# Another order for the tasks of a head pair, on five in-order engines

## The reference

```python
def attention(x, Wq, Wk, Wv, Wp, bp, rel_table):          # 16 heads of 64
    bias = rel_table[clip(rel + 16, 0, 32)]                # rel = key position - query position
    q, k, v = (einsum('btc,hcd->bhtd', x, W) for W in (Wq, Wk, Wv))
    scores = q @ k.T / sqrt(64) + bias                     # causal mask
    return (softmax(scores) @ v).reshape(B, T, 1024) @ Wp + bp

def ffn(x, W_r, W_k, W_v, mu_r, mu_k):
    x_prev = x shifted by one token
    xr, xk = mu_r * x + (1 - mu_r) * x_prev, mu_k * x + (1 - mu_k) * x_prev
    return sigmoid(xr @ W_r.T) * (square(relu(xk @ W_k.T)) @ W_v.T)

x = x + layernorm(attention(layernorm(x), ...))
x = x + layernorm(ffn(layernorm(x), ...))
```

## Time and profile before

| | before |
|---|---|
| median of 3 runs | 2538.27 us (2537.19 to 2540.73) |
| the profiled execution | 2540.03 us |
| its span, first to last instruction | 2538.2 us |
| TensorE products busy | 2326.0 us, 92% |
| VectorE busy | 1971.8 us, 78% |
| ScalarE busy | 1652.5 us, 65% |
| GpSimd busy | 1494.0 us, 59% |
| mean granted TensorE clock | 0.979 |
| chain that ended last | PE 63%, DVE 16%, ACT 13%, issue 7% |

### The profile page before, as it was taken

How to read it: one execution, slowest core, us unless ns; L and a number is a source line. 1 busy time by engine, 2 the same in 40 slices (tenths; PEclk the granted TensorE clock), 3 DMA queues, 4 the chain that set the end, 5 groups by cost and what they waited for, 6 DMA issues and landing times.

```text
span 2538.2 us, 81004 instructions
## 1 busy us (share of the span) xinstructions
PE 2326.0 (92%) x29568; PEld 1533.4 (60%) x29568; DVE 1971.8 (78%) x3848; ACT 1652.5 (65%) x2524; POOL 1494.0 (59%) x2593
## 2 busy tenths in 40 slices
PE   3888989999999999999999999999999999999886
PEld 1454556666656666666666666666666666666575
DVE  6777777888878888788887878778888887777746
ACT  2576666666766766666666676676676666666653
POOL 2233335666666676676666666666667665555652
PEclk8899989999999999999999999999999999999998
DMA  6011111111111111111111111111111111111130
GB/s 156 26 39 39 37 45 49 53 52 59 58 55 56 48 52 58 59 54 58 52 53 50 60 54 61 55 47 52 61 58 54 58 51 48 50 54 53 55 111 20
DMA packets 182457, 140.35 MB, mean 55 GB/s; under 512 B 10400, under 2 KB 173088, under 8 KB 182048
## 3 DMA queue, kind: packets, MB, share of 16 engines
q1 hardware_dynamic: 182048, 134.98, 17.4%
HBM read 57.81 MB, written 43.06 MB: 40 GB/s over the span
## 4 chain that ended last, share of the span: by engine, by line
PE 63%; DVE 16%; ACT 13%; issue 7%; DMA 0%; DVEq 0%; ACTq 0%; POOL 0%; POOLq 0%
PE score_ps L606 12%; PE misc L689 8%; PE misc L562 7%; ACT probs_f L953 6%; DVE row_max L1212 5%; PE misc L670 5%; PE max_ps L628 5%; PE misc L672 4%; PE misc L671 4%; PE misc L577 4%; PE score_ps L610 4%; DVE probs L1196 3%; ACT probs L971 2%; DVE score_ps L1228 2%; PE misc L714 2%
## 5 line engine op out<-in xcount | busy, mean ns | idle before, releaser
L1583 POOL TENSOR_TENSOR probs<-probs_f,probs 128x1024 f16<-128x1024 f32 (+1 forms) x320 | 616.5, 1934 | 517.8 <-ACT probs L971 517.7
L1212 DVE TENSOR_REDUCE row_max<-max_ps 128x2 f32<-128x1024 f32 (+2 forms) x640 | 632.5, 1005 | 81.2 <-PE max_ps L636 81.0
L953 ACT ACTIVATE score_ps<-score_ps,score_unit 128x1024 f32<-128x1024 f32 (+3 forms) x448 | 351.7, 785 | 339.1 <-DVE score_ps L1228 339.1
L953 ACT ACTIVATE probs_f<-score_ps,score_unit 128x1024 f32<-128x1024 f32 (+1 forms) x320 | 329.5, 1030 | 326.6 <-DVE score_ps L1228 281.7
L670 PEld LDWEIGHTS misc<-v_pair,probs 128*128 128x128 f16 x4608 | 419.9, 98 | 75.9 <-issue 53.0
L1196 DVE TENSOR_TENSOR probs<-score_ps,probs 128x1024 f16<-128x1024 f32 (+3 forms) x448 | 375.3, 838 | 115.0 <-ACT probs L971 114.3
L670 PE MATMUL misc<-v_pair,probs 128*128 128x65 f16 x4608 | 452.0, 195 | 0.9 <-issue 0.8
L671 PE MATMUL misc<-v_pair,probs 128*128 128x64 f16 x4608 | 450.4, 194 | 0.0
L672 PE MATMUL misc<-v_pair,probs 128*128 128x65 f16 x4608 | 449.2, 194 | 0.8 <-issue 0.8
L671 PEld LDWEIGHTS misc<-v_pair,probs 128*128 128x128 f16 x4608 | 422.6, 98 | 4.2
L672 PEld LDWEIGHTS misc<-v_pair,probs 128*128 128x128 f16 x4608 | 422.8, 98 | 1.0 <-issue 1.0
(11 more groups left out here) (166 smaller groups left out, 4054.3 us busy)
## 6 DMA issues: line engine op xcount, KB each, us to landing
v_pair<-v_calc SPq DMA_DIRECT2D x64, 516.0 KB, 3.6
o_scratch<-o_stage SPq DMA_DIRECT2D x128, 256.0 KB, 2.3
o_cur<-o_scratch SPq DMA_DIRECT2D x56, 512.0 KB, 3.4
xh<-x SPq DMA_DIRECT2D x56, 128.0 KB, 2.1
x_res<-x SPq DMA_DIRECT2D x56, 128.0 KB, 2.1
out<-out_sb SPq DMA_DIRECT2D x56, 128.0 KB, 1.7
shift_all<-shift_row SPq DMA_DIRECT2D x256, 1.0 KB
probs<-wqkv SPq DMA_DIRECT2D x1, 3072.0 KB, 13.4
```

What stands on the lines that cost most here:

```text
L953: nc.scalar.activation(dst, score_ps[t % 2][:, :, 0:width], ACT.Exp, scale=score_unit[:]).then_inc(exp_done, 1)
L1212: last = dve.tensor_reduce(dst[:, :, i % 4:i % 4 + 1], max_ps[:, :, col:col + width], AX.X, ALU.max)
L1583: pool.tensor_tensor(low, copy_of(par + ahead, t)[:, 0:2 * width], high, ALU.subtract).then_inc(lo_done_pool, 1)
```

## The change

Every engine's list gets another order, and eight of the seventeen tasks change their bank: o2, k0, ot1 and xt go from bank 0 to bank 1, and ffn, q1, v1 and rk from bank 1 to bank 0. No operation is added or left out.

```diff
-TASKS = [("o2", 0, "prev"), ("ffn", 1, "ffn"), ("o3", 0, "prev"), ("q0", 1, "qkv"), ("o0", 1, "att"),
-         ("v0", 0, "qkv"), ("q1", 1, "qkv"), ("k0", 0, "qkv"), ("o1", 1, "att"), ("x2t", 0, "mix"),
-         ("k1", 1, "qkv"), ("ot0", 0, "proj"), ("v1", 1, "qkv"), ("ot1", 0, "proj"), ("proj", 1, "proj"),
-         ("xt", 0, "xt"), ("rk", 1, "mix")]
+TASKS = [("q0", 1, "qkv"), ("ffn", 0, "ffn"), ("o2", 1, "prev"), ("ot0", 0, "proj"), ("o0", 1, "att"),
+         ("o3", 0, "prev"), ("ot1", 1, "proj"), ("q1", 0, "qkv"), ("k0", 1, "qkv"), ("v0", 0, "qkv"),
+         ("k1", 1, "qkv"), ("x2t", 0, "mix"), ("o1", 1, "att"), ("proj", 1, "proj"), ("v1", 0, "qkv"),
+         ("xt", 1, "xt"), ("rk", 0, "mix")]
...
                     if has["proj"]:
+                        load_outputs(n, at)
+                    if has["att"]:
+                        load_shift(m, par, 0, 1)
                     if has["xt"] and (not isinstance(m, int) or n > -LEAD):
                         load_head(n + HEAD_LEAD)
...
-                    if has["qkv"] and not isinstance(m, int):
+                    if has["qkv"]:
+                        project_qk("q0", n, pair * P, ring, span)
+                    if has["att"]:
+                        score(m, par, 0, 1, at)
+                    if has["next"]:
                         ring = pe.snap(ring)
...
                         low_probs(m, par, 0, 4)
                         low_probs(m, par, 0, 6)
+                        low_probs(m, par, 0, 7)
                     if has["ffn"]:
                         final(n, par)
                     if has["att"]:
-                        low_probs(m, par, 0, 7)
                         low_probs(m, par, 0, 8)
```

More of the change, by code:

```diff
@@ L732, in body @@
                     if has["att"]:
-                        score(m, par, 0, 1, at)
+                        score(m, par, 0, 2, at)
+                    if has["ffn"]:
+                        tail_value(n, span)
                     if has["prev"]:
                         weigh_values(2, m, par, 1, span)
-                    if has["ffn"]:
-                        tail_value(n, span)
+                    if has["proj"]:
+                        tail_transpose("ot0", n, span)
+                    if has["att"]:
+                        score(m, par, 0, 3, at)
                     if has["next"]:
@@ L740, in body @@
                     if has["att"]:
[L741 removed]
+                        weigh_values(0, m, par, 0, span)
                     if has["prev"]:
                         weigh_values(3, m, par, 1, span)
+                    if has["proj"]:
+                        tail_transpose("ot1", n, span)
+                    if has["att"]:
+                        score(m, par, 0, 4, at)
+                        score(m, par, 0, 5, at)
                     if has["next"]:
                         fill(m, par, 2, at)
[L746 to L747 removed]
                     if has["qkv"]:
[L749 removed]
+                        project_qk("q1", n, pair * P, ring, span)
+                        project_qk("k0", n, pair * P, ring, span)
                     if has["next"]:
@@ L764, in body @@
                     if has["att"]:
-                        score(m, par, 0, 6, at)
-                    if has["qkv"]:
-                        project_qk("k0", n, pair * P, ring, span)
+                        score(m, par, 0, 7, at)
+                        score(m, par, 0, 8, at)
+                    if has["next"]:
+                        fill(m, par, 5, at)
+                    if has["mix"]:
+                        tail_residual_transpose(n, span)
                     if has["att"]:
                         weigh_values(1, m, par, 0, span)
[L770 to L777, removed]
+                        score(m, par, 0, 9, at)
                     if has["next"]:
                         fill(m, par, 6, at)
[L780 to L788, removed]
-                        fill(m, par, 7, at)
-                    if has["att"]:
-                        score(m, par, 0, 9, at)
                     if has["proj"]:
@@ L795, in body @@
                         tail_project(n, span)
-                    if has["next"]:
-                        fill(m, par, 8, at)
                     if has["att"]:
                         score(m, par, 0, 10, at)
+                    if has["next"]:
+                        fill(m, par, 7, at)
+                    if has["qkv"]:
+                        project_v("v1", n, 4 * par + 2, pair // 2 * 2 * P, ring, span)
+                    if has["att"]:
                         score(m, par, 0, 11, at)
+                    if has["next"]:
+                        score(m, par, 1, 0, at)
+                        fill(m, par, 8, at)
                     if has["xt"]:
@@ L1011, in body @@
                         high_probs(m, par, 0, 1)
+                    if has["proj"]:
+                        tail_outputs("ot0", n)
+                    if has["att"]:
                         exponential(m, par, 0, 2)
@@ L1071, in body @@
                         high_probs(m, par, 1, 0)
+                        shift(m, par, 1, 1)
+                    if has["mix"]:
+                        tail_gate(n)
                 rolled(act, span, body)
@@ L1383, in body @@
                         dve.wait_ge(bandT_in, 16 * 4)
+                    if has["att"]:
+                        low_probs(m, par, 0, 0)
+                        add_bias(m, par, 0, 1, at)
+                    if has["qkv"]:
+                        low_part("q0", m, par, at)
                     if has["next"]:
                         maxima(m, par, 1, 0)
+                    if has["ffn"]:
+                        gated(n)
                     if has["att"]:
-                        add_bias(m, par, 0, 1, at)
+                        low_probs(m, par, 0, 1)
+                    if has["prev"]:
+                        outputs(2, m, par, 1)
                     if has["xt"]:
```

151 lines of the change are left out of this document (62 added, 89 removed).

## The result

| | kernel before | kernel after |
|---|---|---|
| median of 6 runs | 2539.3 us (2537.19 to 2540.73) | 2398.62 us (2395.62 to 2400.45) |
| ratio, 95% interval | | 0.9445 [0.9433, 0.9457] |
| profiled execution, span | 2540.0, 2538.2 us | 2398.64, 2396.8 us |

The kernel is faster by 5.5%. The forecast was 2441 us with a range from 2408: the direction was right, and the gain was larger than the range allowed. In the profiled executions it is 141.4 us where 97 were forecast.

A forecast was written before the change was run, and what follows sets the result against it. TensorE's in-order list was taken to bound the kernel. 56 full pairs x (37.1 - 35.5) = 90, plus 7 for early pairs, is 97; 2540.0 - 97 - 1.8 = 2441 us, range 2408 to 2500.

The forecast's parts named there:

- rival A: Removed TensorE waits come back elsewhere because the walk's margins are thin: 36.5 us per pair, 2497 us; chance 20%.
- B: Rival: slower through the hand-over at the pair's end, q0 and o2 late, 37.9 us per pair, 2583 us; chance 6%.
- the clock rule: Small idles cycling through PSUM banks bring half clock back on TensorE: 2.1 us per pair, 2559 us; chance 2%.
- Step 1: TensorE's order and banks: more work between two users of a bank removes waits of 1.00 and 0.34 us per pair.
- Step 2: ScalarE's and VectorE's order, walked through one pair: waits of 0.40 and 0.27 us go too, margins 0.2 to 0.7.
- Step 3: Last transpose of the maxima: VectorE's 3.3 to 3.4 us against TensorE's 3.64, even to 0.1; drain before q0 0.15.
- rival C: The walk is right to the letter, early pairs gain 2.5 us each: 35.1 per pair, 2408 us; chance 9%.
- The stall-free length: Steady pair on TensorE without its 2.0 us of waits: 35.0 us instead of 37.1.
- Step 4: GpSimd: 31.1 of 35.5 us filled; tile 7 ahead of `final` frees tile 10's copy buffer at 27.2, delays hidden.
- Step 5: SyncE: only the order of loads and stores changes, cover 1 to 5 us, cost taken as 0.
- Step 6: Early pairs before the tail work exists: 1 us gained per pair over 7 pairs, 7 us, bounds -10 and +20.
- Step 7: Loop boundaries: the 2.60 us stall at each loop round's start stays; ends of the kernel 0.

The follow-up runs named there:

- Experiment 1: Kernel before, with only the residual transpose moved on TensorE, from in front of fill 5 to behind the score of tile 7: 2494.28 us, 0.982.
- Experiment 8: Kernel after, with every task on the bank it had before and all new orders kept: 2695.13 us, 1.0616 of the kernel before.
- experiment 2: Kernel after, with fill 5 moved behind the residual transpose, so nine stretches of 64-row products instead of eight: 2451.85 us, 0.9654.
- experiment 3: Kernel after, with fill 5 behind the residual transpose and tile 2's scores behind the feed-forward product, ten stretches of 64-row products: 2462.51 us, 0.9694.
- experiment 6: Kernel after, with fill 5 behind the residual transpose (nine stretches) and GpSimd's old list, tile 7's low part behind `final`: 2414.21 us, 0.9511.
- experiment 4: Kernel after, with one extra VectorE copy of 256 columns ahead of the join of the maxima: 2469.11 us, 0.9726.
- experiment 9: Kernel after, with SyncE's list of before, so the o_cur load leaves later: 2430.4 us, 0.9571.

## Why the prediction was right in direction and off in size

- **The bound** was read rightly: TensorE's waits set the pair. Experiment 1 shows it (one wait out, 0.78 us per pair), and no wait on ScalarE or VectorE in every pair is left. Rivals A and D didn't come, nor B, nor the clock rule: with waits of up to 1.40 us at every early pair's last transpose the granted clock stayed at 1.00, where a pair is 32.2 us.
- **Step 1, TensorE's order and banks:** both waits (1.00 and 0.34) went. Experiment 8 shows that the change doesn't work without the new banks, whose gaps I had tabled. (Three of the gaps in the table are 1.1 to 1.2, not two: `ot0` to `o3` belongs to them.)
- **Step 2, the walk:** as far as the waits show it, it held. The margins of 0.2 to 0.7 us were enough, since none of the waits that I had named as signs of a failure (o0, k1, o1, proj, rk) appears in every pair. The walk was better than I trusted it to be, and that is a good part of the error, next point.
- **Step 3, the first of three terms that failed: 0.1 for the join and 0.2 for margins that fail** (with rounding 0.35 per pair). In the steady pairs they measured 0: no wait stands at the last transpose or at the hand-overs. The drain in front of `q0`, taken as 0.15, is 0.2 in every second loop pair, 0.1 in the mean. "Even, to 0.1" at the last transpose was right: a transpose that has waited starts 0.06 us behind the join (experiment 2), here it starts 0.15 behind, so 0.09 us to spare. The allowances weren't read from any row. For a list of fixed lengths where each margin comes out positive, the estimate is the walk itself, which I had as rival C at 9%; the doubt belonged in the range. It would have given 35.15 in place of 35.5, and 49 x 0.35 = 17 of the missed 44 us.
- **The stall-free length, the second term, was mis-sized, 35.0 for 34.68.** I had seen two overlaps, 0.16 and 0.07, and put them down to short products against projections and scores. They go by the kind of the next product: 64 rows against 128. The old 35.0 holds nine stretches and the new pair eight; one stretch costs 0.20 in experiment 3 and 0.12 in experiment 6, so it makes 0.12 to 0.20 of the 0.32. Most of the rest is a wait of the old list that I hadn't counted. Fill 0 starts 0.34 us behind the last 512-column product of tile 0, which is otherwise followed after 0.22:

```profile
1222.20 0.38 PE L610 MATMUL score_ps<-shift_all,shift_unit 64*128 64x512 f16 x2
1222.54 0.40 PE L628 MATMUL max_ps<-k_hi,q_hi 64*128 64x384 f16 x4
```

  That is 0.12 in this pair and 0.03 in the next. The whole term is 49 x 0.32 = 16 us.
- **Step 4, GpSimd:** that tile 7's new place is hidden was right for the ordinary pairs, and it is worth 10 us in the run, 7.9 of them in the four boundary pairs. But I looked only at when GpSimd delivers. What it does to VectorE while it runs I left out: the join is held by tile 8 for 0.06 us, ends with it (1220.34 and 1220.33) and starts only 0.15 us before tile 10 does. In most of the written-out pairs behind the loop it is held longer and takes 0.29 and 0.58 us in turn, and behind the longer ones the transpose waits 0.02. A copy of 0.36 us more of VectorE work would have cost half of the gain, 1.2 us per pair (experiment 4). With that known, rival A deserved its place, with this mechanism instead of mere thin margins.
- **Step 5, SyncE:** 0 for the new order, as predicted, and the old one would have cost 32 us (experiment 9).
- **Step 6, the early pairs, the third term:** forecast 7 us, measured 23.7 at the first output projection, 20.2 of it in the seven pairs themselves (from a mean of 35.07 to 32.19). The walk said 32.4 per pair and measured were 32.2; the stall at the last transpose was up to 1.7 by the walk and measured 1.40:

```profile
308.81 0.33 PE L648 MATMUL max_ps<-ident,row_max 128*128 128x128 f32 x1 [1.40 <-DVE row_max L1217]
```

  I took 1 us per pair for fear of a stretch at the lower clock level behind it. There was none, and that is where most of the gain seems to come from: TensorE's waits in the seven pairs fell only from 31.9 to 28.9 us in all, while the granted clock rose from 0.92 to 1.00, and 0.08 of 35 us is 2.8 us a pair, a rough upper estimate beside the 2.9 measured, since it counts the time in which TensorE waited, too. The stall at fill 7 (1.85 us) went, those of up to 1.40 stayed; that the clock kept its level because of this wasn't tested. Again the walk was at hand and an allowance was put on it: 17 us of the miss.
- **Step 7, the loop boundaries:** the stall stays, as said (3.74 us here, up to 4.5 in the waits, 2.60 in the earlier trace rows). But the four boundary pairs won 1.2 us each, not the 2.35 of the others: 4.5 us of the gain were lost there. The ends cost 1.4 where I said 0, and the last two pairs lost 0.7.

In sum, of the 44.4 us missed: early pairs 16.7, the 49 ordinary pairs 36.6 (115.0 won where 49 x 1.6 = 78.4 were forecast), against that -8.4 for boundaries, the last pairs and the end (4.9 won where 6.4 were forecast, -0.7 where 3.2 were, -1.4 where 0 was, and one pair fewer than the 56, 1.6). That is 44.9; the difference to 44.4 is rounding, above all of the forecast's own sum, 96.6 to 97.

## What to carry to other kernels

When the bounding engine runs a fixed list, walk the new order by rows and let the walk be the forecast: here every margin that came out positive, even at 0.2 us, cost nothing, and the doubt belonged in the range. Count what changes between neighbouring instructions (here, from 64-row to 128-row products), not only the instructions. Order, buffers and load queue are one change: the same new order with the old banks was 6.2% slower than the kernel before, with the old sync queue it lost 32 of 141 us, and a small VectorE operation that comes where GpSimd is running can cost several times its length.

## What the runs showed of the hardware

- TensorE takes 0.10 us more when a 128-row product follows a 64-row one, and as much the other way (0.312 against 0.216 us, kernel after); one more stretch of 64-row products, a switch each way, costs 0.20 (experiment 3) and 0.12 (experiment 6) per pair.
- A VectorE operation of 0.15 us with two inputs in SBUF takes 1.04 to 1.11 beside a running GpSimd operation, and ends with it, when GpSimd's started first. Operations with one input in PSUM are spared in the same traces: in the kernel after (450 to 2240 us) the maxima of 2 x 512 columns take 1.22 us wholly beside a GpSimd low part and 1.22 away from all of them, VectorE's own 1024-column low parts 1.215 and 1.225.
- Each of the four returns to the start of the loop costs this kernel 5.65 us in the mean: 3.9 to 4.7 of stall, 3.5 to 4.3 of it in the branch of TensorE's own queue, where the other engines' branches take 0.04 to 0.06, and up to 2.8 more in pairs with a granted clock below 1.00. What the branch waits for the trace doesn't show.
- Between a short product and the next projection there are 0.2 us more in every second loop pair (0.31 against 0.11, in a few 0.40); TensorE's queue has register operations there, the first of 0.14 us. Written out, the gap is 0.11 in all.

Open: whether fewer than eight stretches would gain more, and whether written-out steps with the old GpSimd list differ; neither was tried. The new orders of ScalarE and VectorE were never run by themselves or taken back, so what they are worth apart from TensorE's isn't shown.
